# Routing in five groups, and the first expert slots inside the attention drain, in a four-stage hybrid layer

## The reference, cut to what matters

```python
x = x + lightning_attention(layernorm(x))     # 4 batches x 512 tokens x 256, 16 heads, chunks of 128
x = x + moe(layernorm(x))                     # 32 experts, at most 7 kept of the top 8, inner width 96
x = x + softmax_attention(layernorm(x))       # 16 query heads, 4 key heads
x = x + moe(layernorm(x))

def moe(x):                                   # the same weights both times
    probs = softmax(x @ gate_weight.T)
    top_vals, top_idx = top_k(probs, 8)
    keep  = shortest run of ranks whose renormalised sum reaches 0.8
    rw    = top_vals * keep / sum(top_vals * keep)
    for e in range(32):
        g, u = split(x @ w_gu[e].T)
        acc += (silu(g) * u) @ w_d[e].T * weight_of(e)
```

## Time and profile before

| | us |
|---|---|
| median of 3 runs (lowest to highest) | 1120.23 (1114.23 to 1120.39) |
| the profiled execution | 1116.81 |
| its span | 1115.0 |
| busy PE / DVE / ACT / POOL | 875.9 / 587.8 / 543.9 / 655.2 |

### The profile page before, as it was taken

One profiled execution on the slowest core, in us unless ns is written; L12 is line 12 of the kernel. 1 busy time (PEld: TensorE's weight loads), 2 busy tenths in 40 slices (PEclk: granted clock), 3 DMA queues, 4 the chain that ended last, 5 costly groups with the idle time before them and its releaser, 6 DMA issues. The chain is left out here.

```text
span 1115.0 us, 20655 instructions
## 1 busy us (share of the span) xinstructions
PE 875.9 (79%) x5504; PEld 663.5 (60%) x5504; DVE 587.8 (53%) x2104; ACT 543.9 (49%) x1071; POOL 655.2 (59%) x652
## 2 busy tenths in 40 slices
PE   5999998872579799997338897988648799999930
PEld 4566666541578699996323353534327688999830
DVE  4566786865263122226846478675623622222664
ACT  6333446630255355554237767676515355555520
POOL 2466658777666677775641020465665557777773
PEclk9999999985699999999669998989888999999975
DMA  9900002222649886784341111126327588676975
GB/s 338 383 4 2 1 24 83 78 83 83 206 158 305 281 259 220 220 259 152 117 132 34 34 34 34 49 88 231 116 106 232 167 304 279 223 222 215 322 246 193
DMA packets 93231, 181.64 MB, mean 163 GB/s; under 512 B 18985, under 2 KB 73788, under 8 KB 92736
## 3 DMA queue, kind: packets, MB, share of 16 engines
q1 hardware_dynamic: 68544, 114.19, 32.0%
q0 software_dynamic: 24576, 66.13, 16.2%
HBM read 96.34 MB, written 92.27 MB: 169 GB/s over the span
## 5 line engine op out<-in xcount | busy, mean ns | idle before, releaser
L1295 POOL DMA_INDIRECT result_rows<-ys,result_slots x288 | 288.2, 1001 | 106.2 <-issue 91.9
L981 POOL DMA_INDIRECT expert_rows<-route_rows,index x224 | 223.6, 998 | 98.8 <-issue 89.3
L1944 ACT ACTIVATE b_probs<-ps 128x1024 f32<-128x1024 f32 x128 | 127.4, 1030 | 42.1 <-PE ps L1794 42.0
L1447 PE MATMUL ps<-w_gu,f_xts 128*128 x576 | 110.2, 336 | 3.3 <-ACT f_xts L1490 1.8
L1447 PE MATMUL ps<-w_gu,g_xts 128*128 x576 | 108.6, 332 | 2.3 <-ACT g_xts L1490 1.5
L1447 PEld LDWEIGHTS ps<-w_gu,f_xts 128*128 128x128 f32 x576 | 95.3, 196 | 5.3 <-issue 5.2
L1447 PEld LDWEIGHTS ps<-w_gu,g_xts 128*128 128x128 f32 x576 | 94.3, 194 | 3.8 <-issue 3.6
L1540 DVE SCALAR_TENSOR_TENSOR f_h<-ps,f_xs,f_gate 128x96 f32<-128x96 f32 x144 | 39.2, 313 | 101.7 <-ACT f_gate L1497 95.7
L1540 DVE SCALAR_TENSOR_TENSOR g_h<-ps,g_xs,g_gate 128x96 f32<-128x96 f32 x144 | 39.1, 313 | 95.3 <-ACT g_gate L1497 94.1
L1806 PE MATMUL ps<-b_probs,b_v_pad 128*32 128x512 f32 x512 | 76.0, 668 | 13.2 <-issue 6.9
L1508 ACT COPY ys<-ps 128x512 f32<-128x512 f32 x144 | 83.8, 582 | 2.0 <-PE ps L1466 1.9
(11 more groups left out here) (361 smaller groups left out, 1827.7 us busy)
## 6 DMA issues: line engine op xcount, KB each, us to landing
parts<-result_rows SPq DMA_DIRECT2D x32, 896.0 KB, 5.1
f_xs<-expert_rows SPq DMA_DIRECT2D x144, 160.0 KB
g_xs<-expert_rows SPq DMA_DIRECT2D x144, 160.0 KB, 2.7
expert_rows<-pad_rows SPq DMA_DIRECT2D x64, 160.0 KB
w_gu<-in_Wgu SPq DMA_DIRECT2D x1, 6144.0 KB, 17.6
expert_rows<-pad_rows SPq DMA_DIRECT2D x1, 5120.0 KB, 40.0
result_rows<-ys,result_slots POOLq DMA_INDIRECT x288, 3.5
f_w_d<-in_Wdown SPq DMA_DIRECT2D x1, 4096.0 KB, 29.7
```

Of the source, the lines that this page charges most:

```text
L981: self.nc.gpsimd.indirect_dma_start(xs, bass.IndirectOffsetOnAxis(self.index[:, f, t, r:r + 1].bitcast(U32), 0), self.x_rows(f)[:, t, :], ...
L1295: self.nc.gpsimd.indirect_dma_start(self.y_dram, bass.IndirectOffsetOnAxis(self.slots[:, i, j:j + 1].bitcast(U32), 0), self.ys[:, i, j, :] ...
L1447: ins = nc.tensor.matmul(ps[:, bank_gu[u % 2], j * GU:(j + 1) * GU], xts[:, u % 2, o:o + P], w_gu[:, k, bass.ds(experts[j] * GU, GU)], sta ...
L1944: nc.scalar.activation(probs[:, u % RING, :, :], ps[:, 2 * (u % 2):2 * (u % 2) + 2, :], ACT.Exp, scale=float(HD) ** -0.5).then_inc(exp_don ...
```

## The change

Five groups in place of four: in f of 4, 4, 3, 3 and 2 tiles, in g of 4, 4, 4, 2 and 2. The steps of a group in lightning are packed into 11 units instead of 15 (`TOGETHER`), so that scatters begin 9 units after the first step instead of 13. Groups 0, 1 and 2 of f start at units 26, 42 and 54 (58 before). The experts' program is made of generators (`Programs`), one step to a slot. In f they run in lightning's own block: slot 0 in unit 65, slot 9 in unit 74, the rest right behind, with no barrier between. `alone` runs g's as before. In the first ten slots pair inputs have one PSUM bank and gate-up products one, later two each (`Banks`). Group 3 of f is routed from slot 1 and group 4 from slot 9; in g from 0 and 8. There are four lists: 24, 20, 22 and 78 tiles in f, 24, 28, 14 and 78 in g. Padding goes out in slots 25 to 32. The hidden is turned in slot u+3 and the down product made in u+4, with three buffers for it. `LATER` is 16: 56 pairs are scattered in f and 16 in the attention's preparation. `BY_ACT` is 34. Buffers of lightning are put in another order, so that the experts' lie over those that are free. In f POOL sends the results of pairs 0 to 6 in slots 21 to 27 and all others behind; in g those of 0 to 3 in slots 6, 7, 8 and 16, and the others from slot 24. Each list is planned with one more set of columns.

```diff
-COVERED = [int(n * TT * RANKS) + (E if n < B else 0) for n in (2, 3, 3.5, B)]
-LATER = 11
+LATER = 16
+THEN_SLOTS = 10
-PHASES = ((1, 24), (2, 28), (3, TILES - 52))
+PLANS = {"f": Plan(4, 4, 3, 3, 2), "g": Plan(4, 4, 4, 2, 2)}
-    BY_ACT = 40
+    THEN = DRAIN - THEN_SLOTS
+    BY_ACT = 34
...
         def steps_at(unit):
-            for f in range(B - 1):
-                step = unit - (f + 1) * UNITS - FINAL
-                if 0 <= step < routing.STEPS:
-                    yield step, f
+            for f in range(BEFORE_THEN):
+                at = unit - routed_at(routing.plan, f)
+                if 0 <= at < len(Routing.TOGETHER):
+                    for step in Routing.TOGETHER[at]:
+                        yield step, f
...
+            slots = then.tensor(pe)
             for u in range(UNITS, UNITS + DRAIN):
                 finish(u // QUADS, u % QUADS, B - 1)
                 route(UNITS * (B - 1) + u)
+                if u >= UNITS + THEN:
+                    advance(slots)
+            run_all(slots)
...
-    STEPS = 15
-    PLACED = 13
+    TOGETHER = ((0, 1), (2,), (4,), (5,), (6,), (7,), (8,), (9, 11), (10, 12), (13,), (14,))
+    PLACED = len(TOGETHER) - 2
...
+def routed_at(plan, f):
+    return 4 * (plan.ends[f] + 2) + 2
+
+def in_order(begins, plan):
+    order, at = {}, 0
+    for f, done, ready in begins:
+        at = max(at, 2 * ready)
+        for k in range(done, RANKS * plan.sizes[f]):
+            order.setdefault(at // 2, []).append((f, k))
+            at += 1
+    return order
...
-                if 0 <= u - 2 < PAIRS:
-                    turn_hidden(u - 2)
-                if 0 <= u - 3 < PAIRS:
-                    down(u - 3, held.pop(u - 3))
+            if 0 <= u - 3 < PAIRS:
+                turn_hidden(u - 3)
+            if 0 <= u - 4 < PAIRS:
+                down(u - 4, held.pop(u - 4))
...
-                for i in slots_of(((2, 5, 1), (17, 21, 2)), slot):
+                for i in slots_of(((2, 5, 1), (17, 23, 2), (23, 24, 1)), slot):
                     yield LATE_PAIRS[i]
...
+                split = Banks(0, 5, (), ((0, 2), (3, 4), (6, 7))) if final else Banks(
+                    THEN_SLOTS, 5, ((0,), (4,), (7, 6)), ((0, 2), (4, 3), (7, 6)))
```

More of the change, by code:

```diff
@@ L11 @@
+from collections import namedtuple
 from contextlib import ExitStack, contextmanager
@@ L621, in _ @@
             batches(body)
+            slots = then.gpsimd(pool)
             for u in range(UNITS, UNITS + DRAIN):
@@ new lines, in experts, with place, from_list @@
+    h_zero, h_ready, h_turned, ht_sb = sem("h_zero"), sem("h_ready"), sem("h_turned"), sem("ht_sb")
+    down_ready, y_ready, pads_stored = sem("down_ready"), sem("y_ready"), sem("pads_stored")
+    out_stored = sem("out_stored")
+    bank_h = banks.hidden
+    bank_route = [ps[:, 1, :]] * 4
+    starts = plan.first_pair
+    assert place_at.at <= RESULTS_AT
+    def place(u):
+        n = max(n for n, start in enumerate(starts) if start <= u)
+        return n, u - starts[n]
+    def from_list(eng, engine, u, first, most):
+        n, at = place(u)
+        if at == 0:
+            routing.wait_tiles(eng, n)
+        return nc.values_load_multi_w_load_instructions(
+            routing.tab[at:at + 1, n, first:first + 2], engines=[engine], min_val=0, max_val=most,
+            skip_runtime_bounds_check_because="the list is clipped to the experts and their rows")[1]
@@ L1365, in from_list, with experts_of, rows_of, sync @@
+    def experts_of(eng, engine, u):
+        return from_list(eng, engine, u, 0, E - 1)
+    def rows_of(sp, u):
+        return from_list(sp, mybir.EngineType.SP, u, 2, STORED - P)
+    def sync(sp):
+        def load(u):
             n, at = place(u)
             if at == 0:
-                routing.wait_tiles(eng, n)
-            return nc.values_load_multi_w_load_instructions(
-                routing.tab[at:at + 1, n, first:first + 2], engines=[engine], min_val=0, max_val=most,
-                skip_runtime_bounds_check_because="the list is clipped to the experts and their rows")[1]
@@ new lines, in store_pads @@
+        def store_pads(first, count):
+            if first == 0:
+                routing.wait_tiles(sp, LAST)
+            rows = nc.values_load_multi_w_load_instructions(
+                routing.pads[0:1, first:first + count], engines=[mybir.EngineType.SP], min_val=0,
+                max_val=DUMMY - P, skip_runtime_bounds_check_because="an expert has at most every token")[1]
+            for row in rows:
+                sp.dma_start(xs_dram[bass.ds(row, P), :],
+                             routing.tables.pad_rows[:, :]).then_inc(pads_stored, 16)
@@ new lines, in gpsimd @@
+    def gpsimd(pool):
+        for u in range(PAIRS + FLUSH):
+            for step, f in steps_at(u):
+                routing.gpsimd(pool, step, f)
+            for f, k in scatters_at(u):
+                routing.scatter(pool, f, k, xs_dram)
+            for v in results_at(u):
+                pool.wait_ge(y_ready, v + 1)
+                results.scatter(pool, v)
+            yield
+        if out_rows is None:
+            results.wait_scattered(pool, PAIRS - LATER)
+    return Programs(sync, tensor, scalar, vector, gpsimd)
```

745 lines of the change are left out of this document (388 added, 357 removed).

## The result

The change makes the kernel slower: 1133.05 us in the median of four runs (1129.03 to 1133.89) against 1117.23 us (1113.22 to 1120.39) of the kernel before beside it, ratio 1.012 with a 95% interval of 1.009 to 1.015. The profiled execution took 1133.36 us against 1116.81, its span 1131.6 us. 1106 was forecast, with 1126 as the upper end.

What follows compares the result with a forecast made beforehand. POOL's chain was taken to bound the kernel, from first scatter to first exponential and again in g; -11 and -3 gave -14 us, profiled 1116.8 to 1103, median 1106, range 1087 to 1126.

Steps and rivals of the forecast that it cites:

- Earlier first scatter: Lightning's loop: packed steps bring POOL's first scatter from 157.37 to about 140; gain 17 us (11 to 21).
- Group 1's index: Lightning's loop: POOL waits 7 us for it instead of 3.5; loss 3.5 us (0 to 10).
- (c): Rival: DVE fills lightning's loop, over 3.7 us a unit, POOL's chain gains nothing; 1114 to 1126, about 1119; chance 0.22.
- The drain and group 3's index: Lightning's drain: gain 8.3 us before group 3, then POOL waits about 10 us for its index (3 to 18).
- (d): Rival: drain slots over 6 us, POOL waits 28 us for group 3's index; 1130 to 1140, about 1133; chance 0.07.
- The end of f: POOL's last result at 491 to 495, PE ends at 499 to 505, the attention's first late result at 506 to 508.
- 10 us for padding DMAs: End of f: the time added to PE's steady slots of 2.83 us for the padding.
- even, minus 1: `LATER`: ten more late scatters, 13 us, before the exponential, offset by a shorter f; up to 13 if PE ends f.
- -11 us at the exponential: Sum of the terms up to the attention's first exponential, expected near 566: 11 us sooner.
- g, -3: In g: POOL's work the same, four pairs sent by 914 instead of three; taken as 3 us gained.
- up to 4 us: End of f: PE's delay as row loads of slot 66 wait for 49 pairs scattered.
- The rule that speaks against the change: By the Trainium skill, some twenty scatters beside a busier DVE would lose up to 2 us each, 40 us; judged hardly borne out.

Runs made afterwards that it cites:

- `act40`: The changed kernel with POOL making the masks up to unit 39 again, as before (`BY_ACT` 40 instead of 34): 1.0189 of the kernel before.
- `before_pack`: The kernel before with the packed routing steps in the first stage alone: 1.0122 of the kernel before.
- `hold10`: The changed kernel with f's expert pairs held back by ten slots, routing where it was: 1.0169 of the kernel before.
- `late11`: The changed kernel with 11 pairs instead of 16 left for the attention: 1.0063 of the kernel before, 1.0055 the second time.
- `g5`: The changed kernel with g as before in full (four groups of four tiles, sums waiting for 44, 58, 65 and 72 pairs): 1.0052 of the kernel before.
- `late11_g5`: The changed kernel with 11 pairs left for the attention and g as it was before: 0.9990 (0.9972 to 1.0008) of the kernel before.
- `single`: The changed kernel with one routing step to a unit in the loop, group 1's scatters three to a unit, f's late POOL powers three slots back: 1.0245 of the kernel before.
- the first eight experiments: Runs on the number of late pairs, POOL's later power, sums from 49 pairs and g's list cut; both kernels took some 190 us longer.
- `after_again`: The changed kernel unaltered, as the mark for the runs beside it: 1.0114 (1.0089 to 1.0140) of the kernel before.
- `before_sum49`: The kernel before with its sums in g waiting for 49 scattered pairs instead of 44: 1.0003 (0.998 to 1.003) of the kernel before.

## Why the prediction was wrong, step by step

**Earlier first scatter, 140 (136 to 146).** It came at 146.7, after a wait of 8.3 us for the index at 145.5. The gain was 10.7 instead of 17: units 33 and 34, where four steps are packed in two, took 10.8 us together (PE's scores of units 33 and 35 start at 129.7 and 140.5), not 8.

**Group 1's index, a wait of 7.** It was 7.5. But its last scatter ended at 262.0, not 252 (the next two, out by 266.5, are group 2's), and PE's first pair came at 267.8, not 259. The loop's 8.4 us had no term in the sum; they were rival (c)'s. (c) was near on the first stage: first scatter at 146, a wait of 10 for group 1, PE's first pair at 270. Its reason was wrong, though. DVE is busy 107.4 of 145 us in the loop, 74%, or under 3 us a unit and not 3.7: it doesn't fill. POOL waits for DVE in the loop and PE for masks and DVE, each in single waits of up to 8.3 us, and in `act40` and `before_pack` POOL's masks stand behind scatters as well, 7 to 8 us more. That the masks cost nothing on either engine was wrong too: ACT's masks are part of what makes the packing bearable.

**The drain and group 3's index.** One wait of 10 us was foreseen, for an index. There were 8.85 and 7.07 us for the variances of two groups, 0.81 for an index (group 4's), and 2.19 and 4.74 inside groups 2 and 3 that the trace puts down to nothing. The term was 6 us short, and its cause another. The steps that a group packs into one slot were weighed for DVE, and not for POOL's order. Slots 0 to 10 took (311.3 - 270.5) / 10 = 4.1 us, as forecast; the step of (d), 5.5 us a slot, was not reached. (d) named 1133 us, close to the 1133.05 measured, but by luck: of its mechanism PE's ending f by itself at 520 and the late results' price took place, while its slow slots and its POOL wait of 28 us did not.

**The end of f: the step that failed most.** The attention's first late result was to come at 506 to 508, 22 us sooner than before; it came at 526.70, 2.2 us sooner. PE was to end f at 499 to 505 and ended at 519.5 with its last down product. In the forecast's own terms: slot 11 was 8 us late (311.3 for 303), slots 11 to 20 took 37 us and not 29, and the rest, with its "10 us for padding DMAs", took 18 above the steady pace (165.3 us from the product of pair 19 to that of pair 71, for 52 slots of 2.83), with the last list's first load only at 397.92. POOL was to send its last result at 491 to 495, it did at 506.9. And the two were taken as even, so that `LATER` was "even, minus 1". In the kernel before PE already ended f: its last gate and up product starts at 518.3, behind POOL's last result at 516.48, with the last hidden turns and down products still to flush. Who ends the stage was to be read there and was not. POOL's next instruction says it outright:

```profile
524.18 0.10 POOL L800 MEMSET b_ln_root<- 128x4 f32 x1 [6.72 <-POOLq L72]
```

It stood 6.72 us at the barrier. So whatever POOL saves behind its last routed rows falls into that wait (14.1 us after, 32.9 us in `hold10`), and ten results more are 12.3 us of late results on the path: 7 to 8 us net by `late11`, since with 11 pairs left POOL would be last. -11 us at the exponential was +6.9, and that with some luck: the last late result had landed 1.2 us after its issue ended, against 4.4 before.

**g, -3.** Counted from g's first product, POOL's end moved 1.8 us the wrong way (257.3 us for 255.5), with a 7.06 us wait for a variance and 4.98 for the second index in it. And POOL was not the only thing at the end: the sums had about 1 us of slack (the add of tile 13 at 1099.5, the loads behind POOL's last result from 1100.4). The change moves their start from 44 to 49 pairs, which the prediction priced for f ("up to 4 us") and not for g. `g5`, with the groups and the sums of before, gives 7 to 8 us back. This term was missing.

**The rule that speaks against the change.** The 224 scatters have 999 ns on average, 998 before, beside a DVE with the packed steps. Among all 512 indirect DMAs the 105 that no DVE instruction overlaps average 975 ns, and the longest, 1.5 to 2.0 us, all stand beside DVE instructions: single ones take up to 1 us more there. The 170 that a DVE copy or cast overlaps average 980 ns. So the trace still doesn't bear out what the Trainium skill says of such DMAs beside DVE copies (3100 ns in place of 620; SBUF — State Buffer, "A bandwidth-pool intuition that's wrong").

**The sum.** -14 was +13 by the ratio (+16.6 between the profiled executions): late results 7, the sums' wait with g's groups 7 to 8, and what is left of loop, drain and five groups is even by `late11_g5`. That evenness hides large opposite terms: packing in the kernel before costs 13 us (`before_pack`), the overlap of pairs and drain is worth 5 (`hold10`), the masks 7 to 8 (`act40`). These prices come from different kernels and needn't add: the third group's smaller size and its place before the drain weren't varied alone, as `single` shows. The 2.5 us between the exponential and g's first product were not traced.

## What to carry to other kernels

Before costing a shorter chain, read for each stage which engine finishes last there, with its flush and the barrier's wait; a chain that ends 5 us ahead of another has nothing to gain, and work pushed out of it into the next stage goes onto the path there (12 us of late results were 7 to 8 us net). Then follow the lead itself, pair by pair: of 22 us 12 were left at pair 19 and 4 at pair 33, behind padding stores that gate the last list. A threshold that follows from the new plan's formula (here how many pairs a sum waits for) is part of the change like any edit: look for every consumer of it. And an engine that is 74% busy can still be stretched by packing, because in-order engines hand each other waits; look at what stands behind a waiting instruction on each of them.

## What the runs showed of the hardware

In the first eight experiments the kernel before took 1305 to 1318 us, though one of the two chips later ran it at 1120. The first stage was as long as ever (the last score product of the changed kernel starts within 2 us of 245.8), but in f and g PE had long waits that the trace puts down to "issue" (nothing that it shows) and to ACT's copies:

```profile
PE ps L1552 <- issue: 37.7, 5, 18.7
PE ps L1563 <- ACT f_hts L1608: 37.5, 13, 17.2
```

(the waits of PE in `after_again`: in all, how often, the longest, us). What caused it stays open. The changed kernel's ratio was about the same there, 1.0114. But the first sum of g no longer waited for a count of pairs (13.5 us behind it in `before_sum49`, 2.5 us at 1120 us), so what a part costs at one pace need not be what it costs at the other.

In every trace read here indirect DMAs that POOL issues back to back come 1.28 us apart, 0.97 on the engine and 0.30 in front of it. And the table load of ACT ahead of an exponential takes 1.28 us, with the exponential 0.01 us behind it: at 583.86 behind a wait, and at 294.29 right behind a copy.
